# First keys loaded by themselves, mixture weights ahead of half the late scan weights, expert choice spread over scan steps, scan states copied by ScalarE, three bias buffers

## The reference

```
xn = layernorm(x)
x  = x + [ (sigmoid(xn Wg') * O) Wo' + xn ]            # O: chunks of 32 rows, S = Q K' * decay mask, O = S V
       + sum_e sigmoid(xn sel_e) * relu(xn keys_e) values_e      # 16 experts of 128, all used
xn = layernorm(x)
x  = x + sum_m comb[:, m] * h_m                        # 4 mixtures, two of them with weight per row
       + (relu(xn w1_e + b1_e) w2_e + b2_e), e = argmax(xn gate_w' + bias)   # 8 experts, one per row
h_m: h_t = a_t h_(t-1) + x_t,  a = 0.001 + 0.998 sigmoid(xn Wd + bd),  x_t = sigmoid(xn Wg + bg) tanh(xn Wv + bv)
```

## Time and profile before

| | |
|---|---|
| median of 3 runs | 1057.78 us (1053.19 to 1065.77) |
| profiled execution, its own time | 1054.81 us |
| its span, first to last instruction | 1053.0 us |
| mean granted TensorE clock | 0.996 |
| busy: PE, DVE, ACT, POOL | 98%, 72%, 60%, 32% |
| DMA | 141.12 MB, mean 134 GB/s |

### The profile page before, as it was taken

How to read it: one execution, slowest core, us unless ns; L and a number is a source line. 1 busy time by engine, 2 the same in 40 slices (tenths; PEclk the granted TensorE clock), 3 DMA queues, 4 the chain that set the end, 5 groups by cost and what they waited for, 6 DMA issues and landing times. The chain is left out here.

```text
span 1053.0 us, 19905 instructions
## 1 busy us (share of the span) xinstructions
PE 1034.3 (98%) x6598; PEld 924.7 (88%) x6598; DVE 753.1 (72%) x1279; ACT 628.4 (60%) x1143; POOL 339.2 (32%) x287
## 2 busy tenths in 40 slices
PE   8999999999999999999999999999999999999997
PEld 6898898988889898898877888899999999888886
DVE  4875755657575565857769988977777776588887
ACT  3554444444454444545565666788898888566664
POOL 2444453444434445353453684000000000372000
PEclk9999999999999999999999999999999999999999
DMA  5307111010110201423056266578877876452203
GB/s 150 103 6 250 41 40 60 0 60 40 40 60 33 75 31 40 171 71 140 20 224 259 69 242 240 176 233 274 276 258 255 285 249 223 180 195 91 88 13 101
DMA packets 74867, 141.12 MB, mean 134 GB/s; under 512 B 9920, under 2 KB 42560, under 8 KB 73792
## 3 DMA queue, kind: packets, MB, share of 16 engines
q1 hardware_dynamic: 66048, 126.45, 35.0%
q0 software_dynamic: 3072, 8.39, 2.3%
q10 hardware_dynamic: 5696, 5.64, 1.6%
HBM read 101.86 MB, written 38.60 MB: 133 GB/s over the span
## 5 line engine op out<-in xcount | busy, mean ns | idle before, releaser
L768 POOL TENSOR_TENSOR acc<-acc,ytmp 128x512 f32<-128x512 f32 x120 | 156.6, 1305 | 248.3 <-ACT ytmp L853 227.2
L1531 ACT ACTIVATE act_o<-ps,scan_bias 128x512 f32<-128x512 f32 x189 | 129.5, 688 | 103.7 <-PE ps L386 98.3
L853 ACT ACTIVATE ytmp<-ps,sel 128x256 f32<-128x256 f32 x256 | 107.6, 472 | 99.6 <-PE ps L1084 99.0
L923 DVE SCALAR_TENSOR_TENSOR hT_l<-ps,hT_h 128x512 fp32r<-128x512 f32 x128 | 87.6, 685 | 105.9 <-ACT hT_h L815 105.7
L1082 PE MATMUL ps<-vals_h,hT_h 128*128 128x256 f32 x512 | 145.2, 284 | 0.8 <-DVE hT_l L923 0.7
L1083 PE MATMUL ps<-vals_l,hT_h 128*128 128x256 f32 x512 | 143.6, 281 | 0.0
L1084 PE MATMUL ps<-vals_h,hT_l 128*128 128x256 f32 x512 | 143.5, 280 | 0.0
L815 ACT ACTIVATE hT_h<-ps 128x512 fp32r<-128x512 f32 x128 | 76.5, 598 | 99.2 <-PE ps L386 99.0
L1676 POOL DMA_INDIRECT late_y<-y_d,pos_i x20 | 23.2, 1158 | 270.2 <-DMA y_d<-y_sb 264.4
L384 PE MATMUL ps<-xT_h,keys_h 128*128 128x512 f32 x256 | 105.0, 410 | 1.1 <-DVE xT_l L425 1.1
L961 DVE SCALAR_TENSOR_TENSOR acc<-ps,sel,acc 128x256 f32<-128x256 f32 x240 | 103.9, 473 | 3.0 <-PE ps L1084 2.9
(11 more groups left out here) (243 smaller groups left out, 2763.1 us busy)
## 6 DMA issues: line engine op xcount, KB each, us to landing
raw<-w SPq DMA_DIRECT2D x78, 512.0 KB, 5.0
x1T<-xT_d SPq DMA_DIRECT2D x16, 512.0 KB, 5.2
comb_b<-comb_d SPq DMA_DIRECT2D x8, 1024.0 KB, 8.6
w_small<-w SPq DMA_DIRECT2D x14, 512.0 KB, 4.9
xs_d<-zeros ACTq DMA_DIRECT2D x1, 4992.0 KB, 19.2
x_d<-x SPq DMA_DIRECT2D x8, 512.0 KB, 4.3
xn_d<-xn SPq DMA_DIRECT2D x8, 512.0 KB, 2.6
xT_d<-nT_h SPq DMA_DIRECT2D x8, 512.0 KB, 2.7
```

The costliest lines, as they stand in the source:

```text
L768: pool.tensor_tensor(dst[:, 2:4, :], acc[:, 2:4, :], ytmp[:, k % 2, :, :], ALU.add).then_inc(acc23, 1)
L853: act.activation(ytmp[:, k % 2, j - 2, :], yb(k, j), ACT.Copy, scale=sel[:, j, k:k + 1]).then_inc(y_23, 1)
L1531: act.activation(act_o[:, i % 2, w, :], ps[:, 3 * (i % 2) + w, :], func, bias=scan_bias[:, w, i:i + 1]).then_inc(act_g, 1)
```

## The change

At the start, expert 0's keys (128 KB) are loaded by a transfer of their own, with the semaphore `k0_in`, ahead of the other three experts of the chunk. ACT's sigmoid of the decay goes from the head of its queue to group 0, between `relu_hi(1)` and `values(1)`; at the head stands a sigmoid of a constant. PE gets two matmuls on zeros more, after the first transposes.

Between stages A and B1, SP stores the mixture rows and issues three of the late weights, then the load of the mixture rows of group 0, then the other three.

The expert choice of the first 28 tiles of 128 rows is made after steps 1 and 2 of group 0, in two parts of 2 and 4 operations, and that of the last 4 tiles after step 5. The eight scans of 32 numbers in `count_blocks` are one of 256, restarted at each expert by a factor 0 (`within`).

The copies into `hstate` of steps 0 to 5 are made by ACT two steps later, ahead of `a_b`; DVE keeps those of steps 6 and 7.

In slot 0, both engines convert the second half of w2 after the second quarter instead of ahead of the first. The bias has three buffers, and its loads go two slots ahead. The ranking of `mix2` moves from slots 0 to 2 to the end of the last slot but one, and its finish, transpose and copy to the last slot.

Declarations of new semaphores are left out:

```diff
@@ line 192 on @@
     y_sb = rc("y_sb", [P, ST, D], F32)
-    b1c = rc("b1c", [P, FJ], F32)
+    b1c = rc("b1c", [P, ROUND, FJ], F32)
     b2b = rc("b2b", [P, D], F32)
@@ line 694 on @@
+            sp.dma_start(expert0(staged("keys0")), expert0(chunks["keys0"][1])).then_inc(k0_in, 16)
+            sp.dma_start(other_keys(staged("keys0")), other_keys(chunks["keys0"][1])).then_inc(w_in[0], 16)
             for name in FIRST_LOADS:
...
             sp.dma_start(gate_b[:], on_all(a["gate_b"])).then_inc(small_in, 16)
-            for name in order[len(FIRST_LOADS):n_a]:
+            for name in order[1 + len(FIRST_LOADS):n_a]:
                 if name == "o":
@@ line 722 on @@
                 sp.dma_start(x1T[:, 1, part, :, :].bitcast(F32), xT1_d[0, part]).then_inc(x1T_in, 16)
-            sp.wait_ge(side_free, freed(GROUPS - 1, "lt") + 1)
-            mixture_store(sp, mix1)
-            sp.wait_ge(comb_st, 16)
             sp.wait_ge(acc_ip, GROUPS)
+            sp.wait_ge(h_lo, E0 * GROUPS)
@@ line 834 on @@
                 relu_hi(g, 1, first)
+                if first:
+                    act.wait_ge(dec_in, 16)
+                    act.activation(decay[:, 0:1], decay[:, 1:2], ACT.Sigmoid).then_inc(dec_s, 1)
                 values(g, 1, first)
@@ line 879 on @@
-            act.wait_ge(dec_in, 16)
-            act.activation(decay[:, 0:1], decay[:, 1:2], ACT.Sigmoid).then_inc(dec_s, 1)
-            act.wait_ge(w_in[0], 16)
+            act.wait_ge(consts, 5)
+            act.activation(decay[:, 0:1], neg_half[:, 0:1], ACT.Sigmoid)
+            act.wait_ge(k0_in, 16)
             act.activation(expert0(keys_h), expert0(staged("keys0")), ACT.Copy).then_inc(k0_hi, 1)
@@ line 1175 on @@
             pe.wait_ge(consts, 7)
-            for _ in range(N_WARM):
-                pe.matmul(ps[:, 5, 0:D], ident[:], zeros[:], start=True, stop=True)
+            def keep_warm(n):
+                for _ in range(n):
+                    pe.matmul(ps[:, 5, 0:D], ident[:], zeros[:], start=True, stop=True)
+            keep_warm(N_WARM)
             for c in range(DC):
...
                 last_mm.then_inc(side_full, 1)
+            keep_warm(2)
             body(0, True, False)
@@ line 1238 on @@
             g = GROUPS - 1
-            sp.wait_ge(h_lo, E0 * GROUPS)
-            for i in range(N_LATE):
+            sp.wait_ge(side_free, freed(GROUPS - 1, "lt") + 1)
+            mixture_store(sp, mix1)
+            for i in range(N_LATE // 2):
                 load_late(i)
+            sp.wait_ge(comb_st, 16)
             sp.wait_ge(acc01, N01 * GROUPS)
...
             load_comb(0)
+            for i in range(N_LATE // 2, N_LATE):
+                load_late(i)
             x1_store(sp, g)
@@ line 1291 on @@
-            def load_b1(n, e):
+            def load_b1(n, k, e):
+                if not (isinstance(n, int) and n < ROUND):
+                    wait_alone(sp, t_ok, FJ * (n - ROUND + 1))
                 if not zero(n):
-                    wait_alone(sp, t_ok, FJ * n)
-                sp.dma_start(b1c[:], a["b1"][bass.ds(e, 1)].rearrange("a p j -> p (a j)")).then_inc(b1_in, 16)
+                    wait_alone(sp, b1_in, 16 * n)
+                sp.dma_start(b1c[:, k % ROUND, :], a["b1"][bass.ds(e, 1)].rearrange("a p j -> p (a j)")).then_inc(b1_in, 16)
@@ line 1328 on @@
                         load_w1_small(r, expert_at(r, ST))
-                if left(r, k) > 0:
-                    load_b1(n + 1, expert_at(r, k + 1))
+                if left(r, k) > 1:
+                    load_b1(n + 2, k + 2, expert_at(r, k + 2))
                 if not small(k) and bigs_left(r, k) > 1:
@@ line 1343 on @@
             raw2_half(0, 1, e)
-            load_b1(0, e)
+            load_b1(0, 0, e)
             all_scattered(sp)
@@ line 1351 on @@
             raw1_half(1, 1, e)
+            load_b1(1, 1, e)
             raw2_half(1, 0, e)
@@ line 1430 on @@
                         pe.wait_ge(side_free, post_use(GROUPS - 1, "lt")[2])
-                        pe.wait_ge(r_hot, 1)
+                        pe.wait_ge(r_hot, 2)
                         hot = onehot[:].rearrange("p t e -> p (t e)")
@@ line 1493 on @@
                         last_mm.then_inc(l2_part, 1)
-                if left(r, k) == 1:
+                if left(r, k) == 0:
                     mixture_transpose(pe, mix2, 2, 7).then_inc(r_ct, 1)
@@ line 1532 on @@
                     act.wait_ge(scan_ok, n - 1)
+                if i >= 2 and not final(g):
+                    act.activation(hstate[:, i - 2:i - 1], h_b[:, i % 2, GT - 1:GT], ACT.Copy).then_inc(hst_a, 1)
                 act.wait_ge(act_g, 3 * n + 3)
@@ line 1559 on @@
-            def relu(n, q, W):
+            def relu(n, k, q, W):
@@ line 1570 on @@
                     act.activation(t32[:, j, 0:W], ps[:, q, (j % 2) * W:(j % 2 + 1) * W], ACT.Relu,
-                                   bias=b1c[:, j:j + 1]).then_inc(t_ok, 1)
+                                   bias=b1c[:, k, j:j + 1]).then_inc(t_ok, 1)
@@ line 1581 on @@
                 n, (_, st) = ROUND * r + k, blocks(r, k)
-                w2_half(n, 1)
+                if not zero(n):
+                    w2_half(n, 1)
                 for q in range(FJ // 2):
-                    relu(n, q, st * P)
+                    relu(n, k, q, st * P)
                     round_e(n, q, st * P)
+                    if zero(n) and q == 1:
+                        w2_half(n, 1)
                     if q == 1 and not small(k) and bigs_left(r, k) > 0:
@@ line 1592 on @@
                     w2_half(n + 1, 0)
-                if zero(r) and k == 2:
+                if left(r, k) == 0:
                     mixture_sigmoids(act, mix2, 2)
-                if left(r, k) == 1:
                     act.wait_ge(r_ct, 1)
@@ line 1636 on @@
                       allow_small_or_imprecise_dtypes=True).then_inc(r_io, 1)
+            pool.memset(within[:], 1.0).then_inc(r_io, 1)
+            pool.wait_ge(r_io, 6)
+            pool.memset(within[:, :, 0:1], 0.0).then_inc(r_io, 1)
@@ line 1709 on @@
-            def choose_expert():
-                r = (P, TILES, E1)
-                dve.wait_ge(r_io, 5)
-                dve.wait_ge(e_bias, 1)
-                dve.wait_ge(side_free, post_use(GROUPS - 1, "lt")[2])
-                link(dve.tensor_tensor(el[:], logits[:, :, M:NL], ebias[:].unsqueeze(1).to_broadcast(r), ALU.add))
-                link(dve.tensor_reduce(rmax[:], el[:], AX.X, ALU.max))
-                link(dve.tensor_tensor(rt1[:], el[:], rmax[:].unsqueeze(2).to_broadcast(r), ALU.is_equal))
-                link(dve.tensor_tensor(rt1[:], rt1[:], w8[:].unsqueeze(1).to_broadcast(r), ALU.mult))
-                link(dve.tensor_reduce(rmax[:], rt1[:], AX.X, ALU.max))
-                dve.tensor_tensor(onehot[:], rt1[:], rmax[:].unsqueeze(2).to_broadcast(r), ALU.is_equal).then_inc(r_hot, 1)
+            def choose_expert(t0, t1, part):
+                n = t1 - t0
+                r = (P, n, E1)
+                some, best, marks = el[:, t0:t1, :], rmax[:, t0:t1], rt1[:, t0:t1, :]
+                if part == 0:
+                    if t0 == 0:
+                        dve.wait_ge(r_io, 7)
+                        dve.wait_ge(e_bias, 1)
+                    link(dve.tensor_tensor(some, logits[:, t0:t1, M:NL], ebias[:].unsqueeze(1).to_broadcast(r), ALU.add))
+                    link(dve.tensor_reduce(best, some, AX.X, ALU.max))
+                else:
+                    link(dve.tensor_tensor(marks, some, best.unsqueeze(2).to_broadcast(r), ALU.is_equal))
+                    link(dve.tensor_tensor(marks, marks, w8[:].unsqueeze(1).to_broadcast(r), ALU.mult))
+                    link(dve.tensor_reduce(best, marks, AX.X, ALU.max))
+                    dve.tensor_tensor(onehot[:, t0:t1, :], marks, best.unsqueeze(2).to_broadcast(r),
+                                      ALU.is_equal).then_inc(r_hot, 1)
...
                 link(dve.tensor_copy(tot[:], ps[:, 7, 256:512].rearrange("p (t e) -> p e t", e=E1)))
-                for e in range(E1):
-                    link(dve.tensor_tensor_scan(incl[:, e, :], ones[:, 0:TILES], tot[:, e, :], 0.0, ALU.mult, ALU.add))
+                link(dve.tensor_tensor_scan(incl[:].rearrange("p e t -> p (e t)"), within[:].rearrange("p e t -> p (e t)"),
+                                            tot[:].rearrange("p e t -> p (e t)"), 0.0, ALU.mult, ALU.add))
                 r = (P, E1, T // SLOT)
@@ line 1791 on @@
                 if half == 0:
-                    dve.wait_ge(hst, n - MC + 1)
+                    dve.wait_ge(hst_v, 2 * g)
                     carry = hstate[:, i:i + 1]
@@ line 1836 on @@
                 if not zero(g):
-                    dve.wait_ge(hst, n - MC + 1)
+                    if i < MC - 2:
+                        dve.wait_ge(hst_a, (MC - 2) * (g - 1) + i + 1)
+                    else:
+                        dve.wait_ge(hst_v, 2 * (g - 1) + i - MC + 3)
+                if i >= 2 and not final(g):
```

(41 more changed lines are left out.)

## The result

The changed kernel took 1084.0 us (median of 4 runs, 1078.7 to 1089.9), beside 1061.8 of the kernel before (4 runs, 1053.2 to 1066.8): ratio 1.026, with an interval of 1.021 to 1.031. It is slower, and the forecast of 1050, with its range of 1043.5 to 1057, was wrong. In a later set of runs the same program took 1049.5.

A forecast was written before the change was run, and what follows sets the result against it. TensorE, busy for 98% of the span, bounds the kernel, so only its holes and clock count. Terms sum to 6.4 us off 1054.8, giving 1048.4, or 1051.4 from the median; forecast the middle, 1050, range 1043.5 to 1057.

The forecast's parts named there:

- Start, 2.4: Kernel start: first key product 0.7 us earlier, and 1.7 us from no low-clock stretch; bounds -0.6 and 3.3.
- First scan group, 1.7: First scan group: 0.7 us from earlier mixture rows ending PE's nT_l wait, 1.0 us from group 1 starting sooner.
- State copies, 0: Scan steps: copies moved from DVE to ACT at 0.20 us each, covered by ACT's slack, so nothing gained.
- Slots, 2.0 + 1.5 + 0.5 - 1.7: Expert slots: gains of 2.0 in slot 0, 1.5 in the small slot, 0.5 from bias buffers; 1.7 lost before the last.
- The hole of the small slot: First small slot: ten mixture operations leave DVE and PE's 1.5 us hole closes; bounds 1.0 and 1.6.
- The bias buffers: Expert slots: 0.5 us gained from four DVE waits that cost PE 1.0 us together; bounds 0 and 1.0.
- Moving the ranking: Slots: 1.5 us gained in the small slot, 1.7 lost when 17 operations delay the last slot's output layer.
- Sum, 6.4: Whole kernel: 2.4 + 0.7 + 1.0 + 2.0 + 1.5 + 0.5 - 1.7 = 6.4 us gained.
- Rival 4: Scan steps: ACT's state copies reach PE through a_b, price 8.4 us, giving 1056.8 or more; chance 0.04.

The follow-up runs named there:

- fourth set: Unaltered changed kernel, and it with one bias buffer, old mixture ranking or VectorE state copies, beside the kernel before on another chip: 1049.5, 1051.7, 1049.5, 1050.3 against 1054.1.
- both kernels paced: Changed kernel and kernel before, each with POOL waiting on act_g before the 32 gathers and last 20 of 32 scatters: 1049.8 and 1053.5 us.

## Why the prediction was wrong

By its own steps, against the profiled execution of the changed kernel where nothing was hit (1048.9, span 1047.1; the sum said 1048.4). Its rows, from the timelines of PE and DVE and from the stretches:

```profile
11.97 0.47 PE L385 MATMUL ps<-xT_h,keys_h 128*128 128x512 f32 x1 [1.23 <-DVE xT_l L426]
...
530.56 0.69 DVE L1891 TENSOR_TENSOR accO<-h_b,comb_b 128x512 f32<-128x512 f32 x1 [1.21 <-DMA comb_b<-comb_d]
...
556.50 0.50 PE L385 MATMUL ps<-x1T,WB_h 128*128 128x512 f32 x1
...
668.18 0.39 PE L1512 MATMUL ps<-w_h,eT_h 128*128 128x256 f32 x1 [0.56 <-DVE eT_l L1943]
671.66 0.39 PE L1512 MATMUL ps<-w_h,eT_h 128*128 128x256 f32 x1 [0.34 <-DVE eT_l L1943]
684.53 0.39 PE L1512 MATMUL ps<-w_h,eT_h 128*128 128x256 f32 x1 [1.00 <-DVE eT_l L1943]
894.62 0.36 PE L1512 MATMUL ps<-w_h,eT_h 128*128 128x256 f32 x1 [0.36 <-issue]
900.48 0.48 PE L385 MATMUL ps<-x1T,WB_h 128*128 x1
```

```profile
11.97:13.17 1.20, 1.20 (x5) 1.02 (x6) 1.09 (x2) 0.00 (x0) 0.00 (x0) 1.00 0.46 140
670.90:674.31 3.41, 3.07 (x26) 2.87 (x25) 3.25 (x6) 3.04 (x5) 0.00 (x0) 1.00 0.73 229
900.00:933.50 33.50, 33.50 (x153) 27.20 (x152) 23.18 (x27) 19.96 (x35) 23.20 (x22) 1.00 0.67 229
```

- **Start, 2.4.** First key product at 11.97 against 12.51, and 1.00 where the clock was 0.50: 0.54 + 1.7 = 2.2. Right. The first 128 KB of keys landed 5.0 us after their issue. By the formula of the Trainium skill, "DMA: Bandwidth & Descriptors" (Anatomy of one DMA), it would have been 2.3; but that section is on transfers issued by GpSimd, and SP issued this one, beside others.
- **First scan group, 1.7.** comb_b lets DVE go at 530.56, forecast 532. Group 1 starts at 556.50 against 560.70, with no wait for x1T. 4.20 gained by there, 2.2 of it at the start: 2.0. Right.
- **State copies, 0.** 1050.3 with them undone, 1049.5 with them in place, 10 runs each. Right within what is measured.
- **Slots, 2.0 + 1.5 + 0.5 - 1.7 = 2.3.** Slot 0: two short waits (0.56, 0.34) in place of 1.95, at 1.00. The last slot's output layer starts at 894.62, 0.5 late in place of 1.7. The hole of the small slot is gone, as forecast. Between them slot 1 has a wait of 1.00 that I had not seen, half-way through its output layer. Stage B2 starts at 900.48 against 906.50: 6.0 gained in all, 1.8 in the slots. Near, partly by errors that cancel. The bias buffers are worth 2.1 (1051.7 with them undone, against 1049.5), where I took 0.5 with an upper bound of 1.0. I priced them by ACT's 6.8 us of waits in the kernel before; with one buffer the changed kernel has 10.9 us of them, the longest 3.6. Moving the ranking is worth nothing (1049.5 with it undone), against 1.5 - 1.7 in the sum.
- **Sum, 6.4.** Span 1047.1 against 1053.0: 5.9, between two single executions in different sets. Side by side the medians say less: 4.6 in the fourth set (1054.1 less 1049.5), 3.7 with both kernels paced. The sum was 2 to 3 us too high, and that 1049.5 lies by the forecast of 1050 is in part luck.
- **Rival 4**, the only slower one, named the sign that came, ACT ending PE's waits in the scan. It came by another road: the cause that the rival gave, ACT's copies reaching PE, costs nothing measurable.

The step that failed is the one from the sum to the number: "the profiled execution took 1054.8", taken with stages B1 and B2 as fixed, PE full from 906.50 to 940.00. That row is a stretch in which it was not hit. In the changed kernel's execution PE's signals came up to 30.6 us late there and B2 lasted 176.2 us in place of 146.5; the prediction put such a wait at nothing without a reason. The warning stood in the text: "runs of one kernel differ by 12.6 us". I used the spread as noise to read chances by. Paced, the same kernel spreads by 4.5 (1051.2 to 1055.7), and unpaced in the fourth set by 5.4; so most of the 12.6 had a mechanism, one that an edit, or a chip, could make larger, and no rival asked for it. The profile offered the candidate: POOL issuing back to back, in the stages where PE needs a signal answered every 1.4 us.

## What to carry to other kernels

When the runs of one program spread by more than their profile explains, look for the cause before pricing an edit, and give it a rival on the slow side. Judge an undo-one experiment only beside the full change on the same chip: here the copies looked guilty on one chip, the mixture and bias edits on a second, and none of them on a third. Long runs of indirect transfers beside a TensorE stream that is closely tied to other engines are worth spacing out by a wait on the consumer's own counter: no cost of it is visible here, and it gave the best version, 0.992 to 0.994 of the kernel before.

## What the runs showed of the hardware

- PE's semaphore changes can arrive up to 31 us behind the products that make them, while ACT's next to them pass in 0.1 us (act_o ends at 954.95, PE starts at 955.00). Seen only during, and up to 5 us after, runs of POOL's indirect transfers at 1.25 to 1.9 us each, and in four of six sets, counting the first result. Gathers at one per 2.8 us had none of it, nor, in one execution, had 32 plain transfers in 17 us at 252 GB/s. A pause of 3.2 us behind eight scatters ended a lateness of 2.3 us.
- With PE standing, POOL's indirect transfers took a steady 0.95 us to issue; beside a busy DVE 0.95 to 1.9.
- In the execution that was hit, the granted clock fell at 928.9, behind idles of 0.63, 0.33 and 0.77 us from 925.5 on, and stayed at 0.50 until 4.6 us behind PE's restart at 955.0. In the one that was not, three short idles of 0.3 to 1.0 us in the slots left it at 1.00.
